# The mixture follows the attention six steps behind and not seven

## The reference, cut to what matters

```python
# x: (2, 1024, 128); layer norm and modulation ahead of each of the two parts
h = layernorm(x) * (1 + ca) + sa
x1 = h + pointwise(causal_conv3(h))                       # "x1"
q, k, v = rope(x1 @ w_qkv);  q, k = elu(q) + 1, elu(k) + 1
attn = (q . cumsum(k v)) / (q . cumsum(k)) @ w_o           # 16 heads, along 1024 tokens
x2 = x1 + sigmoid((x1 - shifted x1) @ w_gate + b) * attn   # "x2"
h2 = layernorm(x2) * ln_g + ln_b
gw = softmax(h2 @ w_moe_gate)                              # mixture: 4 experts, all of them
ffn = sum_e gw[e] * (silu(h2 @ w1[e] + b1[e]) @ w2[e] + b2[e])
x = x + ga * (x2 + ffn)                                    # "x3"
h3 = layernorm(x) * (1 + cb) + sb
# then 2 of 8 experts for each token: route, scatter rows, gelu experts, gather
x = x + gb * ffn_top2(h3)
```

## Time and profile before

| what | before |
|---|---|
| median of 3 runs | 357.59 us (357.24 to 357.61) |
| the profiled execution's own time | 356.21 us |
| its span, first to last instruction | 354.4 us |
| mean granted TensorE clock | 0.923 |
| busy: PE, PEld, DVE, ACT, POOL | 277.4, 217.4, 223.2, 148.0, 123.6 us |
| the chain that ended last: PE, DVE, ACT, DMA, POOL, issue | 54%, 19%, 8%, 6%, 6%, 5% |

### The profile page before, as it was taken

How to read it: one execution, slowest core, us unless ns; L and a number is a source line. 1 busy time by engine, 2 the same in 40 slices (tenths; PEclk the granted TensorE clock), 3 DMA queues, 4 the chain that set the end, 5 groups by cost and what they waited for, 6 DMA issues and landing times.

```text
span 354.4 us, 5008 instructions
## 1 busy us (share of the span) xinstructions
PE 277.4 (78%) x1657; PEld 217.4 (61%) x1657; DVE 223.2 (63%) x710; ACT 148.0 (42%) x280; POOL 123.6 (35%) x145
## 2 busy tenths in 40 slices
PE   1878558866899899899899989999242899999900
PEld 1444234444767587667787869879231689999900
DVE  2269999959469888599854854564750356545306
ACT  3544351458534448144453664443030264533200
POOL 3102481191100230413002343407477605646730
PEclk9989989998699999999999999999755999999975
DMA  7995003000300000000000001001011332221147
GB/s 215 406 388 224 1 3 118 0 0 0 121 0 2 0 3 1 0 3 0 0 2 0 3 27 35 1 3 47 15 53 53 86 84 75 70 68 37 52 136 252
DMA packets 14985, 22.88 MB, mean 65 GB/s; under 512 B 1904, under 2 KB 10224, under 8 KB 14320
## 3 DMA queue, kind: packets, MB, share of 16 engines
q1 hardware_dynamic: 12336, 17.26, 14.6%
q0 software_dynamic: 2048, 4.25, 3.6%
q10 hardware_dynamic: 576, 1.05, 0.8%
HBM read 13.02 MB, written 9.54 MB: 64 GB/s over the span
## 4 chain that ended last, share of the span: by engine, by line
PE 54%; DVE 19%; ACT 8%; DMA 6%; POOL 6%; issue 5%; SPq 1%; POOLq 0%; DVEq 0%; ACTq 0%
PE ps L1195 51%; DVE qp L846 2%; DVE nd L858 2%; POOL line L395 2%; DMA wide<-chosen 2%; DMA proj_sb<-in_proj 2%; PE ps L1216 2%; DVE acc L935 2%; DVE kv L837 1%; DVE st L719 1%; POOL rstd L361 1%; ACT hid L579 1%; DVE phi L819 1%; POOL phi L392 1%; ACT xh L452 1%
## 5 line engine op out<-in xcount | busy, mean ns | idle before, releaser
L1195 PE MATMUL ps<-w_sb,hid 128*128 128x128 f32 x512 | 60.6, 277 | 0.7 <-DVE acc L935 0.7
L1195 PEld LDWEIGHTS ps<-w_sb,hid 128*128 128x128 f32 x512 | 59.5, 194 | 1.8 <-DVE acc L935 0.9
L579 ACT ACTIVATE hid<-ps,s_sb 128x512 f32<-128x512 f32 x64 | 43.3, 686 | 27.7 <-PE ps L1195 27.1
L1195 PE MATMUL ps<-kv,c_sb 128*128 128x512 f32 (+1 forms) x96 | 39.7, 525 | 4.9 <-DVE qp L846 3.8
L395 POOL DMA_INDIRECT line<-h3r,dest_i x32 | 31.3, 977 | 25.7 <-DVE dest_i L1031 17.1
L1195 PE MATMUL ps<-h2h,w1h 128*128 128x512 f32 x80 | 37.0, 463 | 0.5 <-ACT hid L579 0.3
L1195 PE MATMUL ps<-h2l,w1h 128*128 128x512 f32 x80 | 32.5, 407 | 0.0
L1195 PE MATMUL ps<-h2h,w1l 128*128 128x512 f32 x80 | 32.5, 406 | 0.0
L1195 PEld LDWEIGHTS ps<-wd_sb,hid 128*128 128x128 f32 x256 | 29.7, 192 | 0.8 <-ACT hid L273 0.2
L1195 PE MATMUL ps<-wd_sb,hid 128*128 128x128 f32 x256 | 30.0, 275 | 0.0
L846 DVE TENSOR_TENSOR qp<-ps,phi 128x1024 f32<-128x1024 f32 x16 | 19.5, 1220 | 15.9 <-PE ps L1195 15.8
(11 more groups left out here) (200 smaller groups left out, 526.8 us busy)
## 6 DMA issues: line engine op xcount, KB each, us to landing
line<-wuh SPq DMA_DIRECT2D x8, 262.0 KB, 13.1
phi<-line SPq DMA_DIRECT2D x8, 262.0 KB, 2.8
wd_sb<-in_w_down SPq DMA_DIRECT2D x1, 2048.0 KB, 12.3
chosen<-wuh SPq DMA_DIRECT2D x4, 512.0 KB, 11.3
wst<-in_w_up SPq DMA_DIRECT2D x2, 1024.0 KB, 5.0
x_sb<-in_x SPq DMA_DIRECT2D x4, 256.0 KB, 6.9
wst<-in_w SPq DMA_DIRECT2D x1, 1024.0 KB, 8.0
w_sb<-in_w SPq DMA_DIRECT2D x1, 1024.0 KB, 9.9
```

The costliest lines, as they stand in the source:

```text
L579: a_.activation(hid[:, e % 2, u % FC, :], ps[:, B_UP[u % 2], :], ACT.Silu, bias=s_sb[:, c:c + 1]).then_inc(hid_ready, 1)
L1195: return m.matmul(o, l, r, start=start, stop=stop)
```

## The change

`LAG` is 6 and not 7, so expert `e` stands in step `e + 6`, and the loop has 22 steps and not 23. So that the inputs are there, and the parts behind still fit, other lines move by a part of a step. On TensorE `x2_transposes` of block 0 goes ahead of tile 5's `prefix`; in steps with `f == 2` the attention's q and p, the transposes of `xm` and `downs` stand ahead of the ups, and `mix_logits` between the two pairs; `mix_weights_transpose`, `positions` and `mix_bias` stand at the end of steps with `f == 3`; the `h3` transposes and `route_logits` in steps with `f == 1`. On VectorE `ln2` of block 0 goes ahead of tile 5's `attend`, `split2` into the `attend` of tiles 6, 10 and 14, `acc_start` to the start of steps with `f == 0`, and `stats(2)`, `norm3` and the routing move by one to three steps. GpSimd and ScalarE follow.

```diff
-        LAG = BT + 3
+        LAG = BT + 2
...
-                if f == 2 and live(b - 1):
+                if f == 1 and live(b - 1):
                     inv_std(1, b - 1)
...
+                if f == 3 and live(b - 2):
+                    residual3(b - 2)
                 if f == 0 and live(b - 3):
-                    residual3(b - 3)
-                if f == 1 and live(b - 3):
                     inv_std(2, b - 3)
...
                 if f == 3:
                     query(s)
                     silus(0)
+                    if live(b - 1):
+                        mix_exps(b - 1)
...
-                        mix_exps(b - 1)
-                    silus(2)
+                        gwT_evac(b - 1)
                     attended(s)
...
+                if normed is not None:
+                    split2(normed)
                 dve.wait_ge(cum_read, t + 1)
...
-                if f == 1 and live(b - 2):
+                if f == 0 and live(b - 2):
                     acc_start(b - 2)
-                if 0 <= s - LAG - 2 and f != 0:
+                if 0 <= s - LAG - 2 and f != 3:
                     add_expert(s - LAG - 2)
...
+                if f == 1 and b == 1:
+                    ln2(0)
                 if s < TILES:
-                    attend(s)
+                    attend(s, b - 1 if f == 2 and live(b - 1) else None)
...
                 if f == 2:
                     if live(b + 1):
                         qkv(BT * (b + 1) + 3)
-                    ups(0)
-                    if live(b - 3):
-                        transposes(B_D, tiles(h3, b - 3), h3_ready, b - 2, h3T_ps, h3T_ready)
                     attention("qp")
                     if live(b - 1):
                         transposes(B_D, xm, xm_ready, b, h2T_ps, h2T_ready)
+                    downs()
+                    ups(0)
+                    if live(b - 1):
+                        mix_logits(b - 1)
                     ups(2)
-                    if live(b - 3):
-                        route_logits(b - 3)
-                    downs()
                     attention("a")
                 if f == 3:
                     attention("q")
-                    if live(b - 1):
-                        mix_logits(b - 1)
                     ups(0)
                     attention("p")
                     downs()
                     ups(2)
+                    if live(b - 1):
+                        mix_weights_transpose(b - 1)
+                    if live(b - 3):
+                        positions(b - 3)
                     attention("a")
+                    if live(b - 1):
+                        mix_bias(b - 1)
```

More of the change, by code:

```diff
@@ L426, in _ @@
                     split(s)
-                if f == 2 and live(b - 4):
+                if f == 1 and live(b - 4):
                     scatters(b - 4)
@@ L1074, in _ @@
                     rotate(b + 1)
[L1075 to L1083, removed]
+                if f == 3 and b == 0:
+                    feature(b + 1)
                 if s + 1 < TILES and (f != 3 or b == 0):
                     outer(s + 1)
+                if f == 1 and b == 1:
+                    ln2(0)
                 if s < TILES:
-                    attend(s)
+                    attend(s, b - 1 if f == 2 and live(b - 1) else None)
+                if f == 2 and b == NBLK:
+                    split2(LAST)
+                if f == 1 and b >= 2 and live(b - 1):
+                    ln2(b - 1)
                 if f == 0:
@@ L1091, in _ @@
                     if live(b - 3):
-                        dve.wait_ge(x3_ready, b - 2)
-                        stats(2, b - 3, tiles(x_sb, b - 3))
+                        norm3(b - 3)
                 if f == 1:
-                    if live(b - 1):
-                        ln2(b - 1)
                     if live(b + 2):
                         ln1(b + 2)
-                    if live(b - 3):
-                        norm3(b - 3)
                     if b == 2:
                         residual_scales()
-                if f == 2:
-                    if b >= 2 and live(b - 1):
-                        split2(b - 1)
                     if live(b - 3):
                         route_a(b - 3)
+                if f == 2:
                     if b >= 2 and live(b + 1):
                         rotate(b + 1)
+                    if 0 <= s - LAG - 1:
+                        add_expert(s - LAG - 1)
+                    if live(b - 1):
+                        mix_a(b - 1)
                 if f == 3:
+                    if live(b - 1):
+                        mix_b(b - 1)
                     if b >= 1 and live(b + 1):
@@ L1113, in _ @@
                         outer(s + 1)
[L1114 to L1117, removed]
+                    if live(b - 2):
+                        dve.wait_ge(x3_ready, b - 1)
+                        stats(2, b - 2, tiles(x_sb, b - 2))
                     if live(b - 3):
                         route_b(b - 3)
+                        route_c(b - 3)
             route_b(LAST - 1)
@@ L1421, in _ @@
                         pointwise(b + 1)
+                    if b == 1:
+                        x2_transposes(0)
                     attention("p")
-                    if live(b - 1):
+                    if b >= 2 and live(b - 1):
                         x2_transposes(b - 1)
+                    if live(b - 3):
+                        transposes(B_D, tiles(h3, b - 3), h3_ready, b - 2, h3T_ps, h3T_ready)
                     if live(b + 1):
```

29 lines of the change are left out of this document (11 added, 18 removed).

## The result

The changed kernel takes **360.31 us** (median of 6 runs, 358.27 to 363.40) against 357.41 us (6 runs, 356.45 to 359.89) before: a ratio of 1.0102, 95% interval 1.0066 to 1.0138. It is slower by 2.9 us. The forecast was 357.3 us with a range up to 360.2. The profiled execution is the slowest of the six: 363.40 us, a span of 361.3. The profile of the kernel before is of an execution of 356.21 us, so the two profiles lie 7.2 us apart where the medians lie 2.9 apart.

The account below looks back on a forecast made before the run. PE's work plus 9.0 us of its waits bounds tile 8's `prefix` to the last `downs`. Head start -5.0, waits gone -5.0 and new waits +9.6 give -0.4 us: 357.3 us forecast, range 353.8 to 360.2.

Parts of the forecast that it names:

- by starts: Second count: PE's pieces added step by step from tile 8's `prefix` at 100.4, last `downs` ending +0.2 us later.
- tail: Routing, scatter and top-2 part behind the last `downs`: 104.8 us, claimed to stay in order and length.
- Head start: 7.3 - 2.3 = 5.0 us.: Up to tile 8's `prefix`: 7.3 us more work done by then, less its later start, gains 5.0 us.
- The 2.3: Later start of tile 8's `prefix`: 100.4 instead of 98.07 us.
- The lower clock in step 8: Rival, chance 0.24, slower: half clock also from about 95 us on, head start shrinks by 2.0 us, giving 359.3 us.
- Waits that go and come: PE's waits from tile 8's `prefix` to the last `downs`: 5.0 us go, 9.6 us come.
- New waits: Waits of the new order in steps 10 to 20, mostly at block ends, for copies, silus and `add_expert`: 9.6 us.
- The sum of waits: First count of the whole change: -5.0 - 5.0 + 9.6 = -0.4 us.
- The first up: First up product of step 6: starts at about 76.8 us, 1.8 us earlier.
- its 0.7 us: Possible VectorE slowdown beside GpSimd behind tile 8: 0.7 us once or twice, taken as nothing in the sum.
- The waits are hidden: Rival, chance 0.28: waits at the ends of steps 11 to 20 come at half, about 354.2 us.
- Wrong: a clock under 1.00 after 95 us: Sign that would refute the forecast: PE's clock below full after 95 us.

Follow-up runs that it names:

- run 11: Kernel before with useless products in PE's idle times of the prologue and in ten waits behind step 9: 352.2 us, ratio 0.9859.
- run 12: Changed kernel with useless products in the prologue's idle times and in the waits behind step 9, except ahead of block 1's `h3` transposes: 356.88 us.
- run 2: Kernel before with useless PE products in three idle times of steps 6 and 7: 355.01 us, ratio 0.9941.
- run 3: Changed kernel with block 0's `mix_logits` behind both up pairs of step 6 instead of between them: 359.83 us, ratio 1.0075.
- run 1: Changed kernel with 24 useless PE products behind block 0's `xm` transposes, ahead of the first up: 361.54 us, ratio 1.0104.
- run 6: Changed kernel with useless products in PE's prologue idle times over 0.7 us and behind block 0's `xm` transposes: 357.43 us, ratio 0.9997.
- run 5: Kernel before with useless products in every PE idle time over 0.7 us of the prologue: 352.8 us, ratio 0.9906.
- run 9: Changed kernel with useless products in the prologue and in sixteen waits of steps 9 to 20, one place waiting for VectorE to read its bank: 359.25 us.
- run 8: run 6 with block 0's early parts (`x2_transposes`, `ln2`, `split2`) undone: 361.3 us.
- run 4: run 1 with block ends reordered (bias product and `positions` behind the next step's first ups, `downs` and `route_c` later): 361.16 us.
- run 7: run 6 with the block ends reordered as in run 4: 357.55 us, ratio 0.9993.

## Why the prediction was wrong

What the change did, by the stages of the forecast, in us (change against before):

| stage | forecast | profiled executions | full clock (runs 11, 12) |
|---|---|---|---|
| tile 5's `q` to the first up | -1.8 | -2.0 | -1.2 |
| first up to tile 8's `prefix` | +4.1 | +8.1 | +5.9 |
| tile 8's `prefix` to the last `downs` | -2.7, by starts -2.1 | -0.8 | -0.6 |
| sum | -0.4 to +0.2 | +5.3 | +4.1 |
| tail | 0 | -0.2 | +0.1 |

**The step that failed: "Head start: 7.3 - 2.3 = 5.0 us."** The 7.3 us of work are right (by the counts of the two traces, 934 and 882, 12 up products, 32 of `downs` and 8 rows of the bias product fewer lie behind tile 8's `prefix`). The 2.3 is not: tile 8's `prefix` comes 6.1 us later against tile 5's `q` in the profiled executions (-2.0 + 8.1), and 4.8 at the full clock, so the head start is 1.2 us, or 2.5 there, instead of 5.0. The forecast set 23.6 us for the new order, with the lower clock for the first ups alone, against 19.49 us for the old one, of which 3.3 were the lower clock's (run 2). It so measured the new order against a stage that the lower clock around the old order's waits, 4.71 us the longest, had made longer, and counted little for the clock that follows the new order's own wait of 2.92. At one clock for both, 22.1 us stand against 16.2. Where the lower clock did end at 84.9 us (run 3), the stage took 24.27: the sum of pieces was fair, its clock was not.

**The rival "The lower clock in step 8"** had the right cause and sign and the wrong place: the clock was low from 77.7 to 91.3 us and full from 91.3 on, where the rival set it from 95 on. It cost 3.9 us more than the 23.6, not 2.0. That the clock stays up with products in the wait ahead of the first up, and that the stage then takes 22.1 us, is shown by run 1, and by runs 6 and 12. How the lower clock falls in the five executions without a profile is open. Their lower times (358.27 to 362.41) fit a shorter stretch, as in run 3, but also the differences of the prologue and the tail listed at the end.

**Waits that go and come: right in kind, and the other part of the miss.** Of the 5.7 us between the forecast's -0.4 and the +5.3 of the profiles, 3.8 are the head start and 1.9 are this stage. New waits were put at 9.6 us and measure 10.7: q of step 10 0.73 (0.73 forecast), "a" 0.9 (0.6), bias and `positions` 3.3 (2.85), `downs` 3.2 (3.25), `h3` 1.7 (1.45), `ups(0)` 0.8 in five (0.7 in four). Those that went are 5.3 instead of 5.0. The net, +5.4 of idle time instead of +4.6, leaves 1.1 us: PE is busy for 142.47 - 136.33 = 6.1 us less where 7.3 of work are gone. The sum of waits had no term for this, and "by starts" had it in part. The timelines show 24 waits instead of 16 there. If the loss is theirs, which no run shows by itself, it is an estimated 0.14 us each.

**The other points.** The first up came as forecast by the number, 16.90 us behind tile 5's `q` where 17.1 was forecast, but this is partly luck: `q` was late by the lower clock ahead of it, and VectorE was not. VectorE's `nd` starts 1.46 us ahead of `q` in this profile, and 0.13 behind it in the kernel before and in run 12 (rows below). In run 12 `x2_transposes(0)`, now ahead of tile 5's `prefix`, wait 0.42 us for VectorE's `attT`, and the first up comes 17.52 us behind `q`: 1.2 us are won and not 1.8. It would have been earlier but for the 1.29 us of `h2l`: the Trainium skill, SBUF — State Buffer, section "Who interferes with whom", has the exclusion that would do this, and the rows agree; the forecast had put its 0.7 us behind tile 8 and not here. The tail kept its length. "The waits are hidden" was the wrong way round. The forecast's "Wrong: a clock under 1.00 after 95 us" came out at 1.00: the test was set behind the damage.

`nd` in the kernel before (`q` at 59.67), in the changed kernel (61.47) and in run 12 (60.43), then the wait of run 12:

```profile
59.80 0.29 DVE L863 TENSOR_TENSOR nd<-ps,nd 128x128 f32<-128x128 f32 x1
```
```profile
60.01 0.29 DVE L862 TENSOR_TENSOR nd<-ps,nd 128x128 f32<-128x128 f32 x1
```
```profile
60.56 0.29 DVE L862 TENSOR_TENSOR nd<-ps,nd 128x128 f32<-128x128 f32 x1
63.78 0.63 PE L1282 MATMUL ps<-c_sb,attT 128*128 128x128 f32 x4 [0.42 <-DVE attT L889]
```

So the sign is the order's: 4.6 to 4.7 us by the medians of runs 5, 6, 11 and 12. By the same medians the products win 5.2 us for the old order (357.4 to 352.2) and 3.4 for the new one (360.3 to 356.9); the 1.8 between them is why the change looks smaller in the plain kernels, at 2.9.

## What to carry to other kernels

Starting dependent work earlier pays only by what it takes from idle time; count it from stage lengths at one clock for both orders, and a stage that ran at half the clock before is no measure for a new one. A smaller lag leaves less foreign work to put between an instruction and what it waits for: here a step less exchanged 5.3 us of waits for 10.7. Where PE must wait in a prologue, products into a free bank are worth trying before any change of order: they took the kernel before to 352.2 us, while no median of the order with six steps came under 356.5; give them a bank that no other engine still has to read (run 9).

## What the runs showed of the hardware

- From tile 0's `q` to tile 5's `q` the kernels take 38.2 us at the full clock (runs 5, 11 and 12), and 39.9 in the changed kernel's profile at a mean clock of 0.87. The kernel before takes 38.2 as well, at 0.91: what the lower clock costs depends on where it falls, and a mean clock does not give it. I had read one profile as if its clock were the kernel's. Run 11:

```profile
21.06:59.28 38.22, 32.84 (x167) 20.17 (x168) 35.67 (x56) 14.75 (x36) 13.99 (x10) 1.00 0.36 134
```

- The executions of the kernel before lie between 354.9 and 360.3 us, the six of run 11, with products in its waits, between 351.2 and 353.9. The clock is not all that varies: tile 0's `q` starts at 20.9 to 24.0 us (runs 9 and 8), and the tail behind the last `downs` takes 103.7 to 106.1 (runs 6 and 1), so one profile against another is good to some 1 to 2 us outside the stages compared here.
- Three waits of 0.73, 0.46 and 0.73 us with short work between were followed by a stretch at 1.2 GHz in three profiles (runs 1, 4 and 6) of the seven that have them. In runs 1 and 6 the stage from tile 8's `prefix` to the last `downs`, which holds it, takes 152.4 and 152.2 us, against 150.7 in the plain changed kernel: 1.5 to 1.7 lost. A wait of 1.54 us was followed by it in runs 4 and 7, and the single waits of 0.9 us in the changed kernel's own profile were not. I had looked for the lower clock behind long waits alone. The Trainium skill, TensorE: Matmul & The Clock Gate, Part 1, has the half rate as the default that activity releases; these rows agree.
